# Second cross attention with maxima and products in turn, and multi-query attention rebuilt with one norm and heads in pairs

## The reference

```python
content = einsum('bthd,bThd->bhtT', q + r_w_bias, k)
rel = _relative_shift(einsum('bthd,bThd->bhtT', q + r_r_bias, pe))
attn = (content + rel) * (1.0 / math.sqrt(HEAD_DIM))
attn = attn * mask - 10000000000.0 * (1.0 - mask)
p = softmax(attn); out = einsum('bhtT,bThd->bthd', p, v) @ Wo + bo
```

```python
xn = layer_norm(x, norm_g)          # x is layernorm(x) already
q = xn @ Wq; k, v = split(xn @ Wkv)
q = l2norm(q * 16) * 4; k = l2norm(k) * 4
out = softmax(q k^T) v              # per head
return layer_norm(out @ Wout, out_norm_g)
```

## Time and profile before

| | us |
|---|---|
| median of 3 runs | 1482.43 (1480.89 to 1486.75) |
| the profiled execution, its own time | 1491.19 |
| span of the profiled execution | 1489.4 |
| TensorE matmul / VectorE / ScalarE / GpSimd busy in the span | 1209.5 / 941.3 / 913.0 / 386.6 |
| second cross attention, main block | about 741 to 1308 |
| second cross attention, joining block | about 1308 to 1319 |
| multi-query attention | about 1320 to 1390 |
| mixture of the second block | about 1391 to the end |

### The profile page before, as it was taken

The page is one execution under the profiler, slowest core; times in us unless marked ns, Lnnn a source line. Parts: engine busy times, 40 slices in busy tenths (PEclk is TensorE's granted clock), DMA queues, the critical chain, the costliest instruction groups (busy, mean ns, idle before and its releaser), DMA issues. The chain is left out here.

```text
span 1489.4 us, 25395 instructions
## 1 busy us (share of the span) xinstructions
PE 1209.5 (81%) x8423; PEld 723.6 (49%) x8423; DVE 941.3 (63%) x1573; ACT 913.0 (61%) x1239; POOL 386.6 (26%) x149
## 2 busy tenths in 40 slices
PE   7687777739999868899868888888888888847798
PEld 3334434323344446688624444444444444524587
DVE  5798988951101466622258999999999998535321
ACT  3699999958998335333227777776777777413210
POOL 1000000000000031000017667676676766500000
PEclk9899999978999788899958999999999999556899
DMA  7864544438552330044559888888888888151040
GB/s 261 252 181 106 121 109 121 100 90 155 105 115 57 117 135 1 29 129 153 207 211 327 286 276 288 284 282 286 282 283 282 284 284 278 40 179 42 1 169 8
DMA packets 97049, 257.51 MB, mean 173 GB/s; under 512 B 11193, under 2 KB 41306, under 8 KB 85467
## 3 DMA queue, kind: packets, MB, share of 16 engines
q1 hardware_dynamic: 96992, 256.79, 55.7%
HBM read 165.31 MB, written 91.92 MB: 173 GB/s over the span
## 5 line engine op out<-in xcount | busy, mean ns | idle before, releaser
L1990 POOL TENSOR_TENSOR xb_row<-xb_row,w_mask 128x1024 f32<-128x1024 f32 x128 | 362.0, 2846 | 366.3 <-DVE xb_row L2020 366.3
L2031 DVE CUSTOM_DVE_ANT_0 xb_row<-xb_row,xb_minus 128x1024 f32<-128x1024 f32 x128 | 273.8, 2139 | 37.1 <-POOL xb_row L1990 37.1
L1937 ACT COPY xb_out<-xb_rel_ps 128x1024 f32<-128x1024 f32 x124 | 125.3, 1011 | 98.5 <-PE xb_rel_ps L1822 83.5
L1948 ACT COPY xb_turned<-xb_turn_ps 128x1024 f32<-128x1024 f32 x128 | 129.6, 1012 | 79.4 <-PE xb_turn_ps L1860 78.8
L1860 PEld LDWEIGHTS xb_turn_ps<-_ident,xb_row 128*128 128x128 f32 x1024 | 121.2, 151 | 117.1 <-ACT xb_row L1942 62.8
L1860 PE MATMUL xb_turn_ps<-_ident,xb_row 128*128 128x128 f32 x1024 | 154.6, 299 | 14.0 <-ACT xb_row L1942 11.4
L1822 PE MATMUL xb_cont_ps<-xb_kk,xb_qq 32*128 32x512 f32 x528 | 162.2, 693 | 2.9 <-DVE xb_row L2020 1.5
L2020 DVE TENSOR_TENSOR xb_row<-xb_cont_ps,xb_row 128x1024 f32<-128x1024 f32 x128 | 155.4, 1214 | 11.7 <-PE xb_cont_ps L1822 11.5
L567 DVE TENSOR_REDUCE xa_stats<-xa_b_ps 128x1 f32<-128x1024 f32 x128 | 153.2, 1221 | 12.7 <-PE xa_b_ps L466 12.6
L828 ACT ACTIVATE xa_probs<-xa_psT,xa_t_now 128x1024 f32<-128x1024 f32 x128 | 141.1, 1113 | 25.2 <-PE xa_psT L787 24.9
L1822 PE MATMUL xb_rel_ps<-xb_kk,xb_qq 32*128 32x512 f32 x496 | 148.2, 675 | 4.5 <-ACT xb_out L1937 3.2
(11 more groups left out here) (363 smaller groups left out, 1774.5 us busy)
## 6 DMA issues: line engine op xcount, KB each, us to landing
xb_row<-rel_scores SPq DMA_DIRECT2D x128, 512.0 KB, 5.3
rel_scores<-xb_out SPq DMA_DIRECT2D x32, 1024.5 KB, 5.0
rel_scores<-xb_out SPq DMA_DIRECT2D x32, 1024.0 KB, 4.8
b_e_w<-in_L_ffn_e_w SPq DMA_DIRECT2D x32, 513.0 KB, 3.5
w_w<-in_L_ffn_w SPq DMA_DIRECT2D x24, 512.0 KB, 7.1
xa_k<-first_parts SPq DMA_DIRECT2D x24, 384.0 KB, 5.0
value_rows<-xa_values SPq DMA_DIRECT2D x16, 544.0 KB, 6.1
xb_kk<-key_blocks SPq DMA_DIRECT2D x17, 512.0 KB, 6.3
```

Of the source, the lines that this page charges most:

```text
L1948: nc.scalar.copy(turned[:, part].rearrange("p k n -> p (k n)"), turn_ps[:]).then_inc(turned_sb[part], 1)
L1990: nc.gpsimd.tensor_tensor(row[:, u, at:at + SUB], row[:, u, at:at + SUB], mask[:, t, half * HALF + at:half * HALF + at + SUB], ALU.mult).t ...
L2031: nc.vector.tensor_tensor_reduce(out=row[:, u, at:at + SUB], in0=row[:, u, at:at + SUB], in1=minus[:, t, half * HALF + at:half * HALF + at ...
```

## The change

In `cross1` two orders change, and five weight loads are added to its last block. `multi_query` gets its weights as an argument (`qw`); it makes one norm with the gain, because the layer norm of a layer norm is a norm with another epsilon. The squares move to ScalarE, sums and scaling go by row tile and read the queries from PSUM, the transpositions follow by row tile. `ShortAttention` is replaced by `SidePairs`: the scores are computed with the opposite sign, so that a minimum gives the bias of the exponential directly; the two heads of a pair are issued in turn, and the output projection of a pair is issued two pairs later. The weights of this stage and of the mixture are now kept in SBUF from before they are used to the end of the program, and `latent1` is merged into `middle` with the same number of stages.

The diff, cut to its core:

```diff
@@ -1892,14 +1776,14 @@
                         pe.wait_ge(k_loaded[(c // U + 1) % 2], 16 * (p + (c // U + 1) // 2 + 1))
                     if runs(n, 0):
                         content(p, c, 0)
-                    if runs(n, -2):
-                        turn(p, c - 2, 0)
                     if runs(n, -3):
                         pe.wait_ge(s["sums_sb"], where(p, c - 3)[0] + 2)
                     if makes_queries(n, c, 1):
                         make_queries(p, c)
                     if runs(n, -3):
                         bring_together(p, c - 3)
+                    if runs(n, -2):
+                        turn(p, c - 2, 0)
                     if runs(n, U):
                         relative(p, c + U, 0)
                     if n is not None and n < 0:
@@ -2057,18 +1941,18 @@
                         t = n + NT
                         nc.vector.tensor_scalar(minus[:, t], mask[:, t], 1.0, 1e10, ALU.subtract, ALU.mult
                                                 ).then_inc(s["minus_set"], 1)
-                    if runs(n, -1):
-                        top_of(p, c - 1, 0)
                     if runs(n, -3):
                         sums_out(p, c - 3)
                     if runs(n, 0):
                         add(p, c, 0)
                     if runs(n, -1):
-                        top_of(p, c - 1, 1)
+                        top_of(p, c - 1, 0)
+                    if runs(n, -3):
+                        keep_sums(p, c - 3)
                     if runs(n, 0):
                         add(p, c, 1)
-                    if runs(n, -3):
-                        keep_sums(p, c - 3)
+                    if runs(n, -1):
+                        top_of(p, c - 1, 1)
                     if makes_queries(n, c, 1):
                         make_queries(p, c)
 
@@ -2092,7 +1976,7 @@
 
 
         with ExitStack() as inner:
-            s = {n: f.sem("c_" + n) for n in ("loaded", "dve_steps", "w_in", "w_out", "o_ready", "oT_mm", "oT_sb", "out_mm")}
+            s = {n: f.sem("c_" + n) for n in ("loaded", "next_loaded", "dve_steps", "w_in", "w_out", "o_ready", "oT_mm", "oT_sb", "out_mm")}
             wo = f.sb(inner, "wo", [P, KC, D])
             bo = f.sb(inner, "bo", [P, D])
             bv = f.sb(inner, "bv", [P, KC])
@@ -2111,6 +1995,9 @@
                 sp.dma_start(wo[:], rows_of(i["L1_xattn_Wo"])).then_inc(s["loaded"], 16)
                 sp.dma_start(bo[:], i["L1_xattn_bo"].partition_broadcast(P)).then_inc(s["loaded"], 16)
                 sp.dma_start(bv[:], i["L1_xattn_bv"]).then_inc(s["loaded"], 16)
+                for dst, src in qw.loads:
+                    sp.dma_start(dst, src).then_inc(s["next_loaded"], 16)
+                sp.wait_ge(s["next_loaded"], 16 * len(qw.loads))
 
             @block.vector
             def _(dve):
@@ -2186,20 +2073,158 @@
...
+class QueryWeights:
+    def __init__(self, f, ctx):
...
+        self.loads = [(self.gain[:, n], i[f"L1_attn_{m}"].partition_broadcast(P)) for n, m in enumerate(("norm_g", "out_norm_g"))]
+        self.loads += [(dst[:], rows_of(i[f"L1_attn_{m}"])) for dst, m in ((self.wkv, "Wkv"), (self.wq, "Wq"), (self.wo, "Wout"))]
...
+class SidePairs:
...
+        self.scores = f.ps(ctx, "scores", [P, 4, NT, S])
...
+    def tensor(self, pe, qT, kT, v, behind):
+
+        nc, s, pairs = self.f.nc, self.s, self.heads // 2
+
+        def score(pair):
+            if pair >= 2:
+
+                pe.wait_ge(s["exp_done"], 2 * pair - 2)
+            for t in range(NT):
+                for side in range(2):
+                    rows = slice(side * HD, (side + 1) * HD)
+                    mm = nc.tensor.matmul(self.scores[:, (2 * pair + side) % 4, t], qT[rows, pair, t * P:(t + 1) * P],
+                                          kT[rows, :], start=True, stop=True)
+            mm.then_inc(s["scored"], 1)
+
+        def turn(h):
+            pe.wait_ge(s["normed"], h + 1)
+            if h >= 2:
+                pe.wait_ge(s["probsT_sb"], h - 1)
+            for k in range(NT):
+                for t in range(NT):
+                    mm = nc.tensor.transpose(self.probsT_ps[:, h % 2, k, t * P:(t + 1) * P],
+                                             self.normed[:, h % self.DEEP, t, k * P:(k + 1) * P], self.f.ident[:])
+            mm.then_inc(s["probsT_mm"], 1)
+
+        def weigh(pair):
+            pe.wait_ge(s["probsT_sb"], 2 * pair + 2)
+            if pair >= 2:
+                pe.wait_ge(s["attn_sb"], pair - 1)
+            for k in range(NT):
+                for side in range(2):
+                    mm = nc.tensor.matmul(self.attn_ps[side * HD:(side + 1) * HD, pair % 2, 0:S], v(k),
+                                          self.probsT[:, (2 * pair + side) % self.DEEP, k], start=(k == 0), stop=(k == NT - 1))
+            mm.then_inc(s["attn_mm"], 1)
+
+        score(0)
+        for pair in range(pairs):
+            if pair + 1 < pairs:
+                score(pair + 1)
+            turn(2 * pair)
+            if pair >= 1:
+                weigh(pair - 1)
+            turn(2 * pair + 1)
+            if pair >= 2:
+                behind(pair - 2)
+        weigh(pairs - 1)
+        behind(pairs - 2)
+        behind(pairs - 1)
+
+    def scalar(self, act):
+        nc, s = self.f.nc, self.s
+        for n in range(self.heads + 2):
+            h = n
+            if h < self.heads:
+                b = h % self.DEEP
+                act.wait_ge(s["max_ready"], h + 1)
+                if h >= self.DEEP:
+                    act.wait_ge(s["normed"], h - self.DEEP + 1)
+                for t in range(NT):
+                    ins = nc.scalar.activation(self.probs[:, b, t], self.scores[:, h % 4, t], ACT.Exp, scale=-1.0,
+                                               bias=self.ntop[:, b, t:t + 1], accum_out=self.z[:, b, t:t + 1])
+                ins.then_inc(s["exp_done"], 1)
+            h = n - 2
+            if 0 <= h < self.heads:
+                act.wait_ge(s["probsT_mm"], h + 1)
+                if h >= self.DEEP:
+                    act.wait_ge(s["attn_mm"], (h - self.DEEP) // 2 + 1)
+                nc.scalar.copy(self.probsT[:, h % self.DEEP], self.probsT_ps[:, h % 2]).then_inc(s["probsT_sb"], 1)
+
+    def vector(self, dve):
+        nc, s = self.f.nc, self.s
+
+        def top(h):
+            b = h % self.DEEP
+            dve.wait_ge(s["scored"], h // 2 + 1)
+            if h >= self.DEEP:
+                dve.wait_ge(s["exp_done"], h - self.DEEP + 1)
+            nc.vector.tensor_reduce(self.ntop[:, b], self.scores[:, h % 4], AX, ALU.min).then_inc(s["max_ready"], 1)
+
+        def normalize(h):
+            b = h % self.DEEP
+            dve.wait_ge(s["exp_done"], h + 1)
+            nc.vector.reciprocal(self.rz[:, b], self.z[:, b]).then_inc(s["rz_ready"], 1)
+            dve.wait_ge(s["rz_ready"], h + 1)
+            if h >= self.DEEP:
+                dve.wait_ge(s["probsT_mm"], h - self.DEEP + 1)
+            for t in range(NT):
+                ins = nc.vector.tensor_scalar(self.normed[:, b, t], self.probs[:, b, t], self.rz[:, b, t:t + 1],
+                                              None, ALU.mult)
+            ins.then_inc(s["normed"], 1)
+
+        def keep(pair):
+            dve.wait_ge(s["attn_mm"], pair + 1)
+            nc.vector.tensor_copy(self.attnT[:, pair], self.attn_ps[:, pair % 2, 0:S]).then_inc(s["attn_sb"], 1)
+
+        top(0)
+        top(1)
+        for h in range(self.heads):
+            normalize(h)
+            if h + 2 < self.heads:
+                top(h + 2)
+            if h >= 4 and h % 2 == 0:
+                keep(h // 2 - 2)
...
```

249 lines of the change are left out of this document (59 added, 190 removed).

## The result

The kernel after takes 1440.37 us (median of 4 runs, 1436.97 to 1446.76), the kernel before, run beside it, 1484.59 us: ratio 0.9704, 95% interval 0.9653 to 0.9756. That is 44 us less where 62 were forecast. It is 20 us over the forecast of 1420: inside the stated range of 1400 to 1464, but outside the 1403 to 1437 that the prediction gave its own mechanism. The profiled execution took 1446.76 us, 6 us over the median; its span is 1445.0.

What follows compares the result with a forecast made beforehand. It took the exclusion between GpSimd's products and VectorE's maxima to bound the cross attention's loop. Savings of 44 us there and 18 in multi-query attention took 1482.4 to 1420 us; range 1400 to 1464, own mechanism 1403 to 1437.

Steps and rivals of the forecast that it cites:

- The lock and its chain: Second cross attention: GpSimd's products and VectorE's maxima exclude each other, closing a chain of 8.11 us a slot before the change.
- Base of 7.1 us a slot: Cross attention's loop after the change: a chain through GpSimd over two slots, 7.09 us each, sets the slot.
- the first chain: Cross attention's slot: exponential, transposition, scores, add 1 and maximum 1, ending 6.97 us after the previous maximum 1.
- I add 0.06: Cross attention: new queries delay the transposition some 0.25 us in one slot of four; 0.06 a slot, bounds 0 to 0.28.
- Clock dips: Cross attention's loop: 1.2 us for each of 11 low-clock stretches, 13 us in all, 0.2 a slot, bounds 0 and 0.4.
- TensorE's edit taken as free: Cross attention: half 0's transposition moves behind the gather, starting at E+2.36, E being maximum 1's end; no separate cost.
- DMA: Cross attention: transfers of 6.7 us a slot do not bound; read-backs have 1.8 us of cover, gone if landings together exceed 12.1.
- the lost lock: Rival in the cross attention: the product takes the lock before the maximum, slots of 9.45 us, 1543 us total; chance 0.05.
- Transfers or slow clock: Rival in the cross attention: late landings or clock dips make the slot 7.8 us, total 1446 us; chance 0.17.
- another wait that keeps 8.1 us: Rival in the cross attention: the new order has no effect on the slot, total 1464 us; chance 0.07.
- Multi-query attention: The rebuilt stage behind the cross attention: shorter norms, scaling, transpositions and attention, 18 us saved, bounds 9 and 24.
- If the lower level again lasts 17 us: Multi-query attention with projection: TensorE's lower clock lasts 17 us, giving 29 us; -5 taken, bounds +2 and -10.

Runs made afterwards that it cites:

- e5: Kernel before, with each maximum a plain reduction of the row alone (no mask term, no writing back of the row): 1425.6 us, ratio 0.9594.
- e3: Kernel after, with TensorE's transposition of half 0 back ahead of the wait, VectorE's new order kept: 1416.7 us, ratio 0.9534.
- e1: Kernel after, with both order edits of the cross attention's slot undone, leaving the rebuilt multi-query attention: 1457.3 us, ratio 0.9809.
- e4: Kernel after, with VectorE's order of before, TensorE's new order kept: 1476.6 us, ratio 0.9942.
- e2: Kernel after, with ScalarE's copy of the next query weights moved ahead of the exponential: 1408.6 us, ratio 0.9485.
- e9: e2 with each maximum a plain reduction of the row alone, as in e5: 1399.7 us, ratio 0.9404.
- e6: Kernel after, with the multi-query attention's matmuls of two heads issued head after head instead of alternating: 1434.35 us.
- e8: e2 plus 16 thrown-away matmuls in three TensorE pauses (7 before the projection, 5 during the norm, 4 before the transpositions): 1402.6 us, ratio 0.9441.
- e7: e2 with TensorE's last weighing and relative scores moved behind the next slot's first content scores: 1404.8 us, ratio 0.9475.
- e11: e7 with e8's thrown-away matmuls, 3 instead of 7 in the first place, and 3 more during the first exponentials: 1400.4 us, ratio 0.9413.

## Why the prediction was right in sign and 20 us short

- **The lock and its chain** were right: product and maximum exclude each other through the second operand (e5), alternating them leaves no maximum over 1.68 us, and VectorE's order alone is worth 41 us (e3 against e1; 36 by after against e4) where 44 were forecast for the stage.
- **Base of 7.1 us a slot**: right. The 45 slots without query products average 7.10 us in the kernel after. Without the late weights it is 7.15 (e2), often alternately 7.1 and 7.2 as a chain over two slots makes it; the first chain's 6.97 is seen as 6.95 in e9.
- **The step that failed** is "I add 0.06 (in one slot of four the new queries delay the transposition by some 0.25; bounds 0 to the whole 1.1 us of those matmuls, 0.28 a slot)". The query slot took 2.4 to 4.2 us longer than its neighbours, 0.6 to 1.0 us a slot, beyond the upper bound. Over 59 slots the two terms, 0.06 and 0.2, were to cost 15 us and cost 49.6 in the profile (468.7 us against 59 x 7.10). Of these 34 are the wait (14 x 2.45, the four slots at the upper clock), where 3.5 were forecast and 17 were the bound. Only the length of the matmuls was priced, and not what they wait for. Their input is ScalarE's copy, and the same change had moved the exponential, which stands ahead of that copy, to the end of the slot. The prediction put `make_queries` ahead of the moved transposition and did not ask when its wait ends. e2 gives it back: 32 us.
- **Clock dips** (0.2 a slot, 13 us): the size was about right, the place was not. The other 15 of the 49.6 us are the ten slots with a dip, 11.1 us instead of 9.55. They sit in that same step: in e2 there is no dip from 900 to 1200 us. The runs' spread fits this: e6, with three dips instead of ten, is 11 us shorter in the same loop.
- **TensorE's edit taken as free**: part of the same failure. It costs 19 to 24 us, and pays only with the early copy (e2 at 1408.6 against e3 at 1416.7).
- **DMA**: right for this kernel, and partly by luck. The landings rose from 5.3 and 5.0 to 5.5 and 5.3, and no add waited for a read-back, but the mean slot was 7.94 us and not 7.36. In e2, with the slot near the forecast, they are 6.2 and 5.8, together 12.0 against the 12.1 at which the prediction has the cover gone. There 13 adds wait for read-backs, 15.7 us in all, seven of them from 900 to 1200 us:

```profile
DVE xb_row L1904 <- DMA xb_row<-rel_scores: 6.1, 7, 1.0
```

- **Rivals**: the lost lock did not come. At 993.75 a maximum was issued 0.3 us before product 0 ended, with product 1 released too; it lasted 1.43 us (row below), so it went ahead of the product. Transfers or slow clock (a slot of 7.8 us, 1446) came nearer in number than the forecast, but for another reason: no landing was late, and the dips cost 15 us where 12 were already counted. The miss is the wait, which no rival named. The last one, another wait that keeps 8.1 us (1464), is the nearest in kind.

```profile
993.75 1.43 DVE L1915 CUSTOM_DVE_ANT_0 xb_row<-xb_row,xb_minus 128x1024 f32<-128x1024 f32 x1
```

- **Multi-query attention**: norm 3.5 us (forecast 3.5), products to scaled queries 4.9 (4.9), to the first scores 2.05 (-1.8, forecast -2), final norm 3.7 (-1.6, as forecast), products 0.7 us shorter, not forecast. Attention with projection took 20.5 us instead of 33.4: -12.9 against -5 and a bound of -10. That two heads cost what one does was right (1.14 us for two, 1.13 for one before). The mis-sized term is "If the lower level again lasts 17 us": it lasted 4 of them (0.50 from 1321 to 1325, 0.96 behind). By the prediction's own sum 4 us at the lower level give 22.5 us (4, then 14 of work, 1.5 of gaps and an end chain of 3). The -5 stands for 28.4 us, so the clock makes some 6 of the 8 us between forecast and measurement; for the other 2 the gaps and the end chain were put too long. Before, TensorE stood nearly still for 8.4 us ahead of its transpositions; after, the pause is 2.4 us. That this is why the lower level was short is not shown by a run of its own; e8, with this pause and two others filled, has the first scores at the upper level.

The two errors have opposite signs: 27 us missing in the loop, 9 more in the attention, by the medians of e1 and after (17 for 44, 27 for 18). That is 18 of the 20 us over the forecast; the other 2 are the kernel before, 1484.6 beside this run and 1482.4 where the forecast was laid off. So 9 us of the first miss were hidden by a second one, which is luck: without it the time would be about 1449.

Open: why the granted clock halves in some query slots and not in others after the same pause of 2.2 to 2.4 us, what of e7's slot of 7.91 us is which matmul, and what more than late read-backs disturbs single heads of e2 and e9. None was tried.

## What to carry to other kernels

When a producer moves to the end of a slot, list everything behind it in its engine's queue, and who on another engine waits for each, above all the instructions that come only in one slot of several. Price such a rare step by when its wait ends, not by its own length. And undo each half of a reordering by itself: here one half gave 36 to 41 us and the other took 19 to 24.

## What the runs showed of the hardware that was not expected

- A maximum with two SBUF operands and a product that both wait for the end of a product: the maximum went first each time. In the profile of the kernel after it was issued during a product, with the next product right behind, 46 times, and lasted 1.21 to 1.57 us. Which rule decides is open.
- Matmuls of two heads on different row groups cost the same whether they alternate or come head after head: 1.14 us in e6 against 1.14, with a matmul of each head starting together in both (13 ns apart in e6, 7 in the kernel after).
- Thrown-away matmuls of 4 to 9 us in TensorE's pauses had the granted clock at 1.00 from 7 us behind the last gather on instead of 23 (e8 against e2). After a pause of 1.8 us it fell back for about 3 us; with that pause filled (e11) it did not.
